# Products with unread results on TensorE during its waits, in a two-layer attention and expert kernel

## The reference, cut to what matters

```python
x = x + L0_xattn(layernorm(x), ctx)   # 16 heads of 32; keys and values from ctx, causal
x = x + L0_ffn(layernorm(x))          # 8 experts, 512 -> 2048 -> 512, gelu, top 2
x = x + L1_xattn(layernorm(x), ctx)   # 16 heads of 64; own keys and 722 memory keys
x = x + L1_ffn(layernorm(x))          # 8 experts, 512 -> 1024 (gate, up) -> 512, silu, top 2
```

## Time and profile before

| | us |
|---|---|
| median of 3 runs | 1776.33 |
| lowest, highest | 1775.66, 1778.78 |
| profiled execution | 1778.84 |
| its span, first to last instruction | 1777.1 |
| PE busy in the span | 1589.1 (89%) |
| PE weight loads | 1393.7 (78%) |
| DVE busy | 1146.8 (65%) |
| ACT busy | 835.3 (47%) |
| mean granted clock of PE | 0.939 |

### The profile page before, as it was taken

How to read it: one execution, slowest core, us unless ns; L and a number is a source line. 1 busy time by engine, 2 the same in 40 slices (tenths; PEclk the granted TensorE clock), 3 DMA queues, 4 the chain that set the end, 5 groups by cost and what they waited for, 6 DMA issues and landing times. The chain is left out here.

```text
span 1777.1 us, 32676 instructions
## 1 busy us (share of the span) xinstructions
PE 1589.1 (89%) x12160; PEld 1393.7 (78%) x12160; DVE 1146.8 (65%) x2109; ACT 835.3 (47%) x1546; POOL 253.5 (14%) x300
## 2 busy tenths in 40 slices
PE   6998489999999579979999999999999749999990
PEld 5785378888888569779888887888888549999990
DVE  3686657777777552247676766767676557767774
ACT  2443245555555432246565554646554325445541
POOL 1112201111111010221111111111111031011003
PEclk8998689999999879989999999999999769999995
DMA  6996256666666444240111111020112046666643
GB/s 187 356 392 221 59 209 219 214 203 214 210 205 210 124 159 157 84 128 19 49 44 36 49 27 52 21 61 20 57 30 84 12 146 212 202 205 198 219 155 90
DMA packets 93131, 246.06 MB, mean 138 GB/s; under 512 B 32870, under 2 KB 39526, under 8 KB 77926
## 3 DMA queue, kind: packets, MB, share of 16 engines
q1 hardware_dynamic: 82534, 219.87, 36.8%
q0 software_dynamic: 10496, 24.81, 5.9%
HBM read 179.14 MB, written 65.50 MB: 138 GB/s over the span
## 5 line engine op out<-in xcount | busy, mean ns | idle before, releaser
L1885 PE MATMUL banks<-a_ch,a_wm 128*128 128x362 f32 (+1 forms) x1024 | 286.2, 341 | 9.4 <-DVE a_cl L2046 9.4
L1172 DVE TENSOR_TENSOR e_lo<-e_raw,e_hi 128x2048 fp32r<-128x2048 f32 x98 | 225.4, 2300 | 91.0 <-ACT e_hi L1250 91.0
L1123 PE MATMUL banks<-e_xh,e_hi 128*128 128x256 f32 x768 | 216.4, 282 | 4.2 <-DVE e_xl L1188 4.2
L1123 PE MATMUL banks<-e_xl,e_hi 128*128 128x256 f32 x768 | 216.4, 282 | 0.0
L1123 PE MATMUL banks<-e_xh,e_lo 128*128 128x256 f32 x768 | 216.0, 281 | 0.0
L1250 ACT CAST e_hi<-e_raw 128x2048 fp32r<-128x2048 f32 x98 | 186.4, 1902 | 29.0 <-PE banks L1102 29.0
L1885 PEld LDWEIGHTS banks<-a_ch,a_wm 128*128 128x128 f32 x1024 | 186.5, 191 | 10.9 <-DVE a_cl L2046 10.6
L1885 PE MATMUL banks<-a_cl,a_wm 128*128 128x362 f32 (+1 forms) x512 | 169.2, 331 | 0.0
L1074 POOL DMA_INDIRECT token_sums<-e_y,e_dest x32 | 74.4, 2325 | 600.4 <-DVE e_y L1226 315.4
L1102 PE MATMUL banks<-e_hi,e_hh 128*128 128x512 f32 x384 | 153.8, 401 | 1.5 <-DVE e_hl L1208 1.5
L1123 PEld LDWEIGHTS banks<-e_xh,e_hi 128*128 128x128 f32 x768 | 145.8, 190 | 10.6 <-issue 4.6
(11 more groups left out here) (279 smaller groups left out, 3344.4 us busy)
## 6 DMA issues: line engine op xcount, KB each, us to landing
e_raw<-wout SPq DMA_DIRECT2D x50, 1024.0 KB, 5.0
e_raw<-w SPq DMA_DIRECT2D x34, 1024.0 KB, 21.9
slot_rows<-a_zero SPq DMA_DIRECT2D x66, 514.0 KB, 9.9
e_raw<-wgate SPq DMA_DIRECT2D x17, 1024.0 KB, 4.9
e_raw<-wup SPq DMA_DIRECT2D x17, 1024.0 KB, 4.9
a_craw<-ctxT SPq DMA_DIRECT2D x32, 361.0 KB, 6.8
e_xs<-slot_rows SPq DMA_DIRECT2D x18, 514.0 KB, 3.7
p_raw<-Wkv SPq DMA_DIRECT2D x4, 1024.0 KB, 13.2
```

The costliest lines, as they stand in the source:

```text
L1123: mm = nc.tensor.matmul(ps[:, bank, 0:CAP], w[:, cc, cut], x[:, cc, :], start=t == 0, stop=t == len(terms) - 1)
L1172: nc.vector.tensor_tensor(lo[g % 2][i], raw[q % RAW][:], hi[g % 2][i].bitcast(F32), ALU.subtract)\
L1885: mm = nc.tensor.matmul(ps[:, 6 + half, 0:wide], w[:, cc, cut], x[:, cc, start:start + wide], start=cc == 0 and t == 0, stop=cc == DC - 1 ...
```

## The change

TensorE is given products whose results nobody reads: a weight tile by itself, 128 x 128 by 128 x 512, into a PSUM bank that is free at that point (bank 7 in `front`, bank 3 in the others), each overwriting the last. They use operands that are complete there. In `front` that is the high part of the output weights, and in the last two places the first weight chunk of the experts, for which a wait on `e_hi` is added; in `project` it is the first chunk `hi[0]`, with a wait on `hi_done`. There are 6 ahead of the value product for b = 6 and for b = 7, then 6, 8, 8 and 10 in the tail; 14 between `turn(0)` and the loop of `experts`, which is called twice; in `project` 12 ahead of the first turn and 5 behind each of the first five. That is 44 + 28 + 37 = 109.

```diff
@@ front, TensorE
+                def idle_products(n, wide):
+
+                    for _ in range(n):
+                        nc.tensor.matmul(ps[:, 7, :], wide[:, 0, 0:128], wide[:, 1, :], start=True, stop=True)
+
...
                         project_half(*block_at(b), 0)
+                    else:
+                        idle_products(6, wo[0])
                     values(b)
...
                     attended(b)
+                idle_products(6, wo[0])
                 route_logits(B - 2)
+                idle_products(8, wo[0])
                 output(B - 1)
                 route_rank(B - 2)
+                pe.wait_ge(e_hi, 1)
+                idle_products(8, ahead0.hi[0])
                 route_turn(B - 1)
                 route_logits(B - 1)
+                idle_products(10, ahead0.hi[0])
                 route_rank(B - 1)
@@ experts, TensorE
                 turn(0)
+                for _ in range(14):
+                    nc.tensor.matmul(ps[:, 3, :], hi[0][0][:, 0, 0:128], hi[0][0][:, 1, :], start=True, stop=True)
                 with pe.Fori(0, n) as j:
@@ project, TensorE
+                def idle_products(n):
+
+                    for _ in range(n):
+                        nc.tensor.matmul(ps[:, 3, :], hi[0][:, 0, 0:128], hi[0][:, 1, :], start=True, stop=True)
+
+                pe.wait_ge(hi_done, 1)
+                idle_products(12)
                 for b in range(5):
                     turn(b)
+                    idle_products(5)
                 for t in range(2):
```

## The result

| | before | after |
|---|---|---|
| median of 20 runs | 1776.95 us | 1772.61 us |
| lowest, highest | 1773.48, 1780.37 | 1767.71, 1776.56 |
| profiled execution | 1778.84 | 1770.84 |
| its span | 1777.1 | 1769.1 |
| PE busy | 1589.1 | 1607.5 |

The ratio of the two is 0.9975, with a 95% interval of 0.9967 to 0.9983: 4.4 us faster (3.0 to 5.9), where 1772.0 was forecast.

What follows compares the result with a forecast made beforehand. Behind the heads TensorE was taken as the bound, losing time at low clock after waits. The terms summed to -5.3 us; less 1.0 for the profiled execution's own stretches, -4.3 gave a median of 1772.0, range 1768 to 1776.5.

Steps and rivals of the forecast that it cites:

- A: Six products ahead of the value product of b = 6 fit its wait and keep the clock high: -1.3 us.
- B: Six products ahead of the value product of b = 7 start at low clock and delay it: +0.6 us.
- C: Products in the first attention's tail: output product starts late but ends 0.3 earlier, rank products gain 0.2: -0.6 us.
- D: Fourteen products in the first experts' head: 1.0 us beyond the wait, 2.6 won from the low stretch: -1.6 us.
- E: Projection's head: twelve products free, five behind each of five turns, low 5.0 us stretch brought to full clock: -2.0 us.
- F: Fourteen products in the second experts' head: 1.35 us late, 1.76 won from the low stretch: -0.4 us.
- fourth rival: In the attention's tail products stay at low clock and delay what DVE waits for: +7.3 us, 1783.6; chance 0.06.
- third rival: In the projection the clock falls again and five products per turn are too few: time 1774.2 us; chance 0.15.
- The rule on transposes: For the projection's head: transposes don't count as TensorE's activity like other products, so don't bring the full clock.
- second rival: Delay eats the gain: low-clock products outlast their waits in B, C, D and F; sum -1.5 us, 1774.8; chance 0.19.

Runs made afterwards that it cites:

- e0_after: The changed kernel once more, unaltered, as a yardstick against the kernel before: 1762.00 against 1764.96 us, ratio 0.9984.
- e11_best: Changed kernel with none ahead of b = 7's value product, 6, 8, 6 in the tail, 9 per experts' head, 17 before projection, additions by DVE: ratio 0.9958.
- e10_bridge: Changed kernel with 17 instead of 12 products ahead of the projection's first turn: 1775.10 us, ratio 0.9991 to the kernel before.
- e3_project: Kernel before plus only the projection's products, 12 ahead of the first turn and five behind each of five turns: 1763.08 us, ratio 0.9986.
- e8_trim_spread: Changed kernel with the fewer products of e4_trimmed and GpSimd's eight additions spread over the first pass: 1759.78 us, ratio 0.9971 to the kernel before.
- e2_experts: Kernel before plus only the 14 products in each of the two heads of the experts: 1764.68 us, ratio 0.9989.
- e12: Kernel before, without added products, with GpSimd's eight additions done by DVE ahead of the second experts' first turn: 1776.56 against 1775.85 us, ratio 1.0003.
- e9: Changed kernel with GpSimd's eight additions done by DVE ahead of the second experts' first turn: 1770.34 us against 1775.85 for the kernel before, ratio 0.9970.
- e1_front: Kernel before plus only the first attention's 44 added products: 1765.40 against 1766.04 us, ratio 1.0000.
- e4_trimmed: Changed kernel with none ahead of b = 7's value product, 6, 8, 6 in the tail, 9 per experts' head: 1760.53 us, ratio 0.9964 to the kernel before.
- e5_transposes: Changed kernel with the 14 products in both heads of the experts replaced by 20 transposes: 1762.64 us, ratio 0.9989 to the kernel before.
- e7_spread: Changed kernel with GpSimd's eight additions in the second experts each behind one block of the first pass: 1761.84 us, ratio 0.9981 to the kernel before.

## Why the prediction was right, and where its terms were not

The forecast was -4.3 us, the result -4.4. That they agree to 0.1 us is luck: the terms are off by up to 1.4 us each, and the same kernel measured again on another chip (e0_after) gave -2.8 (-1.1 to -4.6). The mechanism was right: products with unread results, run in waits, bring the full clock to the work behind. Mean of the profiled executions with a part, less the mean without, against the terms:

| term | forecast (ends) | measured | from |
|---|---|---|---|
| A + B | -0.7 (-2.8, +1.9) | -1.0; +0.5 | "b=6 and 7": 42.2 against 43.2; 35.5 against 35.0 |
| C | -0.6 (-1.0, +2.9) | -0.1 to -0.3 | rest of front: 44.3 against 44.4; 40.6 against 40.9 |
| D | -1.6 (-2.4, +0.6) | -1.7 | 40.1 against 41.8 |
| E | -2.0 (-2.2, +1.0) | -2.2 | 170.4 against 172.6 |
| F | -0.4 (-1.2, +0.9) | +1.0 | 29.4 against 28.4 |

Where two values stand, the first is for the slower chips, the second for the faster. F is counted with GpSimd's additions unaltered. The slower chips' A + B leaves out e11_best, which has A alone. The sums are -4.0 and -2.7 us; measured were -4.4 and, by e0_after, -2.8.

A, B. In A each step came as written in the changed kernel: a wait left of 1.10 for the 1.2 forecast, 1.00 on the clock, the next rank 1.6 us earlier, the good end. But in e10_bridge the clock fell at 149.8 in spite of the six products, which then took 2.81 us. And the reading of the rows was not quite right: in the kernel before the first product at 152.00 took 0.48 us where one at low clock takes 0.75, so the clock was still high through the wait and fell some 0.4 us behind its end. What the sum missed is that the next fall comes sooner. In the kernel before the clock was at 1.00 up to 166, with the low stretch of 152 behind it; after the change it fell at 164.6. On the faster chips it is plainer: e3_project, low between 148 and 152, kept the full clock up to 166, and its b=6 and 7 took 35.75; e8_trim_spread, with A and without B, was high there, fell at 158, stayed low for some 10 us, and took 35.53. And e2_experts, without A, was not low at 148 at all (34.18). The clock of e3_project and e8_trim_spread, by the same views:

```profile
148.00:152.00 4.00, 4.00 (x11) 2.80 (x12) 2.49 (x3) 1.41 (x5) 0.00 (x0) 0.60 1.03 343
158.00:164.00 6.00, 3.58 (x100) 2.99 (x104) 4.92 (x14) 1.91 (x7) 4.96 (x5) 1.00 0.45 138
```
```profile
148.00:152.00 4.00, 4.00 (x24) 3.03 (x23) 3.20 (x7) 1.42 (x7) 0.00 (x0) 1.00 0.90 254
158.00:164.00 6.00, 5.65 (x80) 4.53 (x84) 3.49 (x9) 1.01 (x2) 3.98 (x5) 0.50 0.54 153
```

So in these executions a low stretch taken away was partly exchanged for another. B itself cost some 0.8 us on the slower chips (from the rank at 159.88 to that at 181.10 in the kernel before 21.22, in e12 21.43; with B 22.24, 22.18 and 21.83 in after, e9 and e10; in e11, with A alone, 20.92), near the forecast's +0.6.

C. The output product did start late, and on the first chip it ended later, not 0.3 earlier: in the window 194.80 to 201.40 the clock averages 0.71, so it rose at about 198.6, 7.8 us after the first added product of the tail, later than any of the six rises in the earlier trace rows. The fourth rival's condition ("the rise comes more than about 6 us after the start") thus came true in one place, and cost some 0.8 us at DVE's addition (20.2 us after the rank that ends "b=6 and 7", against 19.5). The ten products before the rank then had full clock and fit (2.54 us); in e1_front it was the other way round: the tail high, the ten low (4.61 us). Either way next to nothing was won with these numbers. With 6, 8 and 6 products in the tail (e4_trimmed, e8_trim_spread) the rest of the front is 39.3 and 39.6 us against 40.9 without any, and in e11_best 43.7 against 44.2 and 44.5: some 1.4 and 0.7 us were to be had with fewer.

D. Mechanism and size right. What the term had as its price, 1.0 us beyond the wait, was nil in the changed kernel (6.16 us from the turn against 6.14; up to 0.4 in e0_after): the clock rose 2.3 us after the first of the 14, not 4.3, and they took 4.53 us instead of 5.2. The term counted from the wrong place: the turn runs right ahead of them, and e5_transposes shows that transposes lift the clock too. From the start of the turn the rise took 3.3 to 5.4 us in the first experts and 2.8 to 4.1 in the second, over all ten kernels with products there, which lies within the prediction's own 2.6 to 5.8. Against that the low stretch it replaced is shorter in most executions than the 5.8 us in the rows (D without products 41.4 to 41.7 three times, 42.65 once).

E. Right, and the third rival is refuted for the profiled execution of the changed kernel; in e3_project, e4_trimmed, e7_spread and e8_trim_spread it was partly at work (first product 46.3 to 47.8 us behind the last turn of the experts instead of 45.9), and took at most 1.9 of the gain. What let the clock fall there was the wait ahead of the first turn (2.52 us in e3_project). The rule on transposes from the Trainium skill, on which that rival leaned too, doesn't hold for this kernel's transposes by e5_transposes.

F. This is the step that failed, and by more than its ends: +1.0. The forecast counted the delay (1.35) and the gain (1.76) and took for granted that behind the head TensorE is the bound. The delay was nil and the full clock came, but the work behind it then ran into DVE (2.11 us of waiting against 0.69), and behind the wait the clock was low again (0.59). The cause is shown by e9_dve_adds against the changed kernel (F 26.76 against 29.4) and e7_spread: DVE's roundings beside GpSimd's additions. With the cause away (e9_dve_adds) F is -1.6, or about -1 with the 0.5 us that the rest of the stage took more there (306.1 against 305.4 to 305.8); in e11_best F is -2.1 against e12_adds_only, with the rest unchanged (305.6 against 305.7). The term's idea was good for that. The forecast read only the rows up to the first useful product and not DVE's first blocks behind it.

The second rival (delay eats the gain) is what happened in the front, in part; the whole gain was larger than its 1.5 us because in D, E and F of the changed kernel the rise came 2.3, 4.2 and 1.9 us after the first added product, not 5.8.

## What to carry to other kernels

Products with unread results pay where dense work on TensorE follows a long wait: here D, behind a wait of 4.2 us, and E, behind 23 us of waiting and a sparse stretch, gave 1.7 and 2.2 us, and nine products did what fourteen did. In a chain where TensorE and another engine hand over to one another (the attention's tail) as many as the waits can take at high clock gave next to nothing, and fewer of them about 1 us; ahead of a wait of under 1 us six cost some 0.8. Before counting a gain from a higher clock, look at what the next engine does in the first blocks behind it: a contention that cost nothing while TensorE was slow (GpSimd's additions beside DVE's roundings) can become the bound.

## What the runs showed of the hardware

- DVE beside GpSimd. A rounding of 128x256 that takes 0.29 us took 1.42, and a subtraction of the same size 1.40 for 0.43, when GpSimd additions of 100x512 (1.32 us for the one in e7_spread) were running. In e7_spread the subtraction at 1438.79 ends at 1440.19, 0.3 us after the addition's end at 1439.90, near its own length: it waited for that end. The Trainium skill, "SBUF — State Buffer", section "SBUF: two separate sides", says that the two engines share a pair of ports which one of them holds for a whole instruction; the trace agrees.
- The same program takes 1776 us on some chips and 1766 on others. The difference lies in the first attention, behind the rank at 138.32 (front 87.3 and 87.9 against 75.2 and 76.6 without products there; that rank itself comes at 137.5 to 139.2 on all). In PE's timeline of the slower chips the sums of the attention (L567) stop several times for 0.15 to 0.86 us on "issue", with nothing in the trace that they wait for (why is open); on the faster ones 32 of them run through in 0.87 to 1.58 us. Slower chip first, then a faster one:

```profile
167.58 0.57 PE L567 MATMUL banks<-a_PT,a_ones 100*32 100x100 f32 x5 [0.15 <-issue]
169.01 0.33 PE L567 MATMUL banks<-a_PT,a_ones 100*32 100x100 f32 x1 [0.86 <-issue]
```
```profile
160.84 1.56 PE L567 MATMUL banks<-a_PT,a_ones 100*32 100x100 f32 x32
```

- From the start of dense work to the rise of the clock there is no fixed time. In one execution, the changed kernel's, it was 3.9 us in D (from the turn on) and 7.8 us in C (from the first added product on, and TensorE had worked before that too). For the same code at the same place, the low stretch ahead of the value product of b = 7, it was back at about 162 in e5_transposes and 168.8 in e0_after:

```profile
162.00:164.00 2.00, 2.00 (x45) 1.37 (x36) 1.59 (x1) 0.00 (x0) 1.14 (x2) 0.94 0.69 211
```
```profile
160.00:168.00 8.00, 8.00 (x98) 6.39 (x91) 5.05 (x4) 1.00 (x2) 2.65 (x3) 0.50 0.46 132
```

The part around it, "b=6 and 7", took 34.19 us in the one and 36.99 in the other. Such differences are a likely source of the several us between two runs of one kernel; no run measured that.
